# Local attention: V evicted on VectorE, q's norm as the exponential's per-row scale, the input split on POOL

## What is computed

```python
def _layer(x, wqkv, qs, ksc, wo, lg, lb, w1, b1, w2, b2):
    h = shift_token(x)
    q, k, v = jnp.split(h @ wqkv, 3, axis=-1)       # 8 heads of 64
    q = l2norm(q) * qs
    k = l2norm(k) * ksc
    q, k = rotary_xpos(q, k)
    o = local_attention(q, k, v)                    # windows of 64, each with the one before it
    x = x + o @ wo
    h = layernorm(shift_token(x)) * lg + lb
    h = h @ w1 + b1
    a, g = jnp.split(h, 2, axis=-1)
    return x + (a * gelu(g)) @ w2 + b2
```

## Time and profile before

| | |
|---|---|
| median of 3 runs | 910.92 us (910.48 to 911.56) |
| the profiled execution's own time | 909.12 us |
| its span on the core | 907.3 us |
| mean granted TensorE clock | 0.98 of full speed |
| busy: TensorE, VectorE, ScalarE, POOL | 89%, 75%, 71%, 59% |
| local loop, 27 passes of layer 1 | 208.58 to 430.86 us |
| local loop, 27 passes of layer 2 | 567.89 to 790.16 us |

### The profile page before, as it was taken

The page is one execution under the profiler, slowest core; times in us unless marked ns, Lnnn a source line. Parts: engine busy times, 40 slices in busy tenths (PEclk is TensorE's granted clock), DMA queues, the critical chain, the costliest instruction groups (busy, mean ns, idle before and its releaser), DMA issues.

```text
span 907.3 us, 26209 instructions
## 1 busy us (share of the span) xinstructions
PE 803.8 (89%) x9912; PEld 616.1 (68%) x9912; DVE 677.0 (75%) x1389; ACT 645.5 (71%) x2037; POOL 531.6 (59%) x529
## 2 busy tenths in 40 slices
PE   4979999779999999999889887999999999988985
PEld 3558777557777777778766555777877777775652
DVE  4788898777887887787466767778787788746765
ACT  1217677579989899889743237988988998964463
POOL 1494233178888888888610008888888888951100
PEclk9999999989999999999999999999999999999998
DMA  7220001012222222222201122222222222222001
GB/s 272 73 52 4 3 4 41 3 48 54 51 64 57 60 51 63 53 63 54 60 19 24 23 52 54 63 55 57 58 61 56 62 51 61 57 51 100 0 35 58
DMA packets 64704, 48.24 MB, mean 53 GB/s; under 512 B 40410, under 2 KB 50948, under 8 KB 64068
## 3 DMA queue, kind: packets, MB, share of 16 engines
q1 hardware_dynamic: 64580, 46.57, 19.9%
HBM read 10.63 MB, written 2.10 MB: 14 GB/s over the span
## 4 chain that ended last, share of the span: by engine, by line
PE 55%; DVE 17%; ACT 17%; issue 7%; POOL 2%; DMA 1%; SPq 0%; DVEq 0%; POOLq 0%; ACTq 0%
PE ps L404 46%; PE ps L414 9%; ACT prob L862 6%; DVE nmax L1124 3%; ACT sq L804 3%; DVE nt L1152 2%; ACT V L831 2%; ACT oT L813 2%; DVE split L952 2%; ACT kT L838 1%; ACT pT L808 1%; DVE prob L1211 1%; DVE split L950 1%; ACT qT L823 1%; DVE vexp L1043 1%
## 5 line engine op out<-in xcount | busy, mean ns | idle before, releaser
L862 ACT ACTIVATE prob<-ps,nmax 128x128 f32<-128x128 f32 x512 | 181.8, 375 | 35.6 <-DVE nmax L1124 35.5
L404 PE MATMUL ps<-wqkv,split 128*128 128x512 f32 x576 | 186.8, 435 | 13.4 <-DVE split L952 9.9
L1349 POOL TENSOR_TENSOR prob<-prob,rinv 128x512 f32<-128x512 f32 x128 | 133.7, 1045 | 87.2 <-DVE rinv L1110 45.8
L404 PEld LDWEIGHTS ps<-wqkv,split 128*128 128x128 f32 x576 | 96.9, 194 | 32.5 <-DVE split L952 10.0
L1124 DVE TENSOR_REDUCE nmax<-ps 128x4 f32<-128x512 f32 x128 | 83.6, 686 | 47.0 <-PE ps L404 47.0
L414 PE MATMUL ps<-ident,prob 128*128 128x128 f32 x640 | 97.8, 276 | 14.1 <-POOL prob L1349 13.2
L862 ACT ACTIVATION_READ_ACCUMULATOR prob<-ps,nmax 128x1 f32 x512 | 109.2, 213 | 0.0
L1360 POOL TENSOR_TENSOR qr<-qr,ss 128x512 f32<-128x512 f32 x64 | 66.9, 1045 | 52.1 <-DVE qr L1136 52.1
L414 PEld LDWEIGHTS ps<-ident,prob 128*128 128x128 f32 x640 | 75.6, 141 | 28.3 <-POOL prob L1349 17.5
L404 PE MATMUL ps<-oT,wo 128*128 128x128 f32 x512 | 73.9, 287 | 22.2 <-ACT oT L813 22.2
L404 PEld LDWEIGHTS ps<-oT,wo 128*128 128x128 f32 x512 | 62.1, 191 | 37.5 <-ACT oT L813 36.5
(11 more groups left out here) (134 smaller groups left out, 1886.3 us busy)
## 6 DMA issues: line engine op xcount, KB each, us to landing
VB<-V SPq DMA_DIRECT2D x129, 128.0 KB, 2.4
kT<-kT SPq DMA_DIRECT2D x65, 128.0 KB, 2.4
XS<-X SPq DMA_DIRECT2D x32, 128.0 KB, 2.3
XS<-X SPq DMA_DIRECT2D x128, 32.0 KB, 1.9
D<-in_xT SPq DMA_DIRECT2D x8, 256.0 KB, 4.9
XS<-in_xT SPq DMA_DIRECT2D x2, 1024.0 KB, 6.3
out_T<-XS SPq DMA_DIRECT2D x8, 256.0 KB, 2.0
raw<-in_wqkv SPq DMA_DIRECT2D x2, 768.0 KB, 3.9
```

Of the source, the lines that this page charges most:

```text
L404: return nc.tensor.matmul(o, l, r, start=start, stop=stop, skip_group_check=True)
L862: nc.scalar.activation(prob[:, par, grp, s * P:(s + 1) * P], ps[:, 4 + grp, s * P:(s + 1) * P], ACT.Exp, bias=nmax[:, par, grp * 4 + s:grp ...
L1349: g.tensor_tensor(p4, p4, rinv[:, slot, 4 * grp:4 * grp + 4].unsqueeze(2).broadcast_to([P, 4, P]), ALU.mult).then_inc(l_prob, 1)
```

## The change

Three things are done together.

1. V's eviction from PSUM bank 2 goes from ScalarE to VectorE. On VectorE it stands behind the sums of squares and ahead of the maxima.
2. The rotated q is no longer multiplied by its inverse norm on POOL. The scores are then those of the unscaled q. The inverse norm, one number a row and head, is given to each exponential as a per-row scale; the negated maximum has to be scaled as well, which is a new VectorE product of 128x4 (`scaled_maxima`) behind each maximum. `ss` gets a third slot, and TensorE's turn of q waits for VectorE's q directly.
3. The input is split per tile of 128 tokens on POOL, at the end of each pass, and no more per chunk of 512 on VectorE every fourth pass.

```diff
 (TensorE)
-                        pe.wait_ge(l_split, L * CHUNKS + (n + 2) // TPC + 1)
+                        pe.wait_ge(l_split, base + n + 3)
...
-                        transposed(n, par, qr, l_qn)
+                        transposed(n, par, qr, l_qr)
 (ScalarE)
-                    if live(n, 0, TILES):
-
-                        act.wait_ge(l_v, base + n + 1)
-                        wait(act, l_o, base + n - 1)
-                        if live(n, -1, TILES):
-                            act.wait_ge(v_prev[nxt], 32 * ((base + n - 1) // 2 + 1))
-                        nc.scalar.activation(V[:, par, :], ps[:, 2, :], ACT.Copy).then_inc(l_ve, 1)
...
-                            wait(act, l_qn, base + n + 1)
-                            wait(act, l_kn, base + n + 1)
-                            nc.scalar.activation(ss[:, par, :], lognt[:, 1, :], ACT.Exp, scale=-0.5).then_inc(l_rnorm, 1)
+                            wait(act, l_kn, base + n)
+                            wait(act, l_max, 2 * (base + n))
+                            nc.scalar.activation(ss[:, (n + 2) % 3, :], lognt[:, 1, :], ACT.Exp, scale=-0.5).then_inc(l_rnorm, 1)
...
                                                      bias=nmax[:, par, grp * 4 + s:grp * 4 + s + 1],
+                                                     scale=ss[:, n % 3, 2 * s + grp:2 * s + grp + 1],
 (VectorE)
-                            v.tensor_reduce(nmax[:, par, 4 * grp:4 * grp + 4],
+                            v.tensor_reduce(rawmax[:, par, 4 * grp:4 * grp + 4],
                                             ps[:, 4 + grp, :].rearrange("p (s k) -> p s k", s=4),
-                                            AX_X, ALU.max, negate=True).then_inc(l_max, 1)
+                                            AX_X, ALU.max, negate=True).then_inc(l_rawmax, 1)
+
+                    def scaled_maxima(grp):
+                        if live(n, 0, TILES):
+                            dve.wait_ge(l_rawmax, 2 * (base + n) + grp + 1)
+                            v.tensor_tensor(nmax[:, par, 4 * grp:4 * grp + 4], rawmax[:, par, 4 * grp:4 * grp + 4],
+                                            ss[:, n % 3, grp:HEADS:2], ALU.mult).then_inc(l_max, 1)
...
+                    if live(n, 0, TILES):
+                        dve.wait_ge(l_v, base + n + 1)
+                        wait(dve, l_o, base + n - 1)
+                        if live(n, -1, TILES):
+                            dve.wait_ge(v_prev[nxt], 32 * ((base + n - 1) // 2 + 1))
+                        v.tensor_copy(V[:, par, :], ps[:, 2, :]).then_inc(l_ve, 1)
                     maxima(0)
-                    if live(n, 3, TILES) and (n + 3) % TPC == 0:
-                        j = (n + 3) // TPC
-                        if j > 1:
-                            dve.wait_ge(l_v, base + n + 3 - TPC)
-                        split_into(j % 2, shifted(XS[0], j, CHUNK), CHUNK, l_split, L * CHUNKS + j)
+                    scaled_maxima(0)
                     maxima(1)
+                    scaled_maxima(1)
 (POOL)
-                        pool.wait_ge(l_qr, base + n + 2)
-                        pool.wait_ge(l_rnorm, base + n + 2)
-                        g.tensor_tensor(hd(qr[:, nxt, :]), hd(qr[:, nxt, :]),
-                                        ss[:, nxt, 0:8].unsqueeze(2).broadcast_to([P, HEADS, HD]),
-                                        ALU.mult).then_inc(l_qn, 1)
...
+                    if live(n, 3, TILES):
+                        m = n + 3
+                        wait(pool, l_v, base + m - 2 * TPC + 1)
...
+                        x_m, slot, cols = shifted(XS[0], m, P), (m // TPC) % 2, bass.ds((m % TPC) * P, P)
+                        g.tensor_copy(split[:, slot, 0, cols], x_m).then_inc(split_hi, 1)
+                        pool.wait_ge(split_hi, base + m + 1)
+                        g.tensor_tensor(split[:, slot, 1, cols], x_m, split[:, slot, 0, cols].bitcast(F32),
+                                        ALU.subtract).then_inc(l_split, 1)
```

More of the change, by code:

```diff
@@ L134, in build @@
         VB = sb("VB", [P, 2, INNER])
-        ss = sb("ss", [P, 2, 2 * HEADS])
+        ss = sb("ss", [P, 3, 2 * HEADS])
+        rawmax = sb("rawmax", [P, 2, HEADS])
         nt = sb("nt", [P, 2 * HEADS])
@@ L235, in build @@
         l_qr = sem("l_qr")
-        l_qn = sem("l_qn")
+        l_rawmax = sem("l_rawmax")
         l_kr = sem("l_kr")
@@ L945, in rstd_links @@
                     ins.then_inc(ln_rstd, 1)
[L947 to L952, removed]
             def centre(base, j, src, bank):
@@ L1131, in local @@
                         v.tensor_tensor(hd(kn[:]), hd(ps[:, 1, :]),
-                                        ss[:, nxt, 8:16].unsqueeze(2).broadcast_to([P, HEADS, HD]),
+                                        ss[:, (n + 1) % 3, 8:16].unsqueeze(2).broadcast_to([P, HEADS, HD]),
                                         ALU.mult).then_inc(l_kn, 1)
@@ L1371, in local @@
                         g.tensor_tensor(kr[:, nxt, :], kA[:], kB[:], ALU.add).then_inc(l_kr, 1)
+                    if live(n, 3, TILES):
+                        m = n + 3
+                        wait(pool, l_v, base + m - 2 * TPC + 1)
+                        if m == 0:
+                            pool.wait_ge(xs_dma, xs_before_local(0) if L == 0 else xs_before_ffn(L - 1) + 32)
+                            wait(pool, ffn_a, NPART * (L * CHUNKS - 1))
+                        elif m == TPC:
+                            pool.wait_ge(xs_dma, xs_before_local(L))
+                            wait(pool, ffn_a, NPART * L * CHUNKS)
+                        x_m, slot, cols = shifted(XS[0], m, P), (m // TPC) % 2, bass.ds((m % TPC) * P, P)
[3 more added lines that the diff above has]
+                                        ALU.subtract).then_inc(l_split, 1)
                     if live(n, 0, TILES):
                         normalise(n, par, 0)
-                steps(-1, TILES - 2, local)
+                steps(-3, TILES - 2, local)
                 local(TILES - 1, 1)
```

## The result

The changed kernel takes 1185.95 us in the median (1180.02 to 1191.21, four runs) against 910.7 us; the ratio is 1.302, with a 95% interval of 1.294 to 1.311. The profiled execution took 1180.02 us, its span is 1178.2 us and its mean granted TensorE clock 0.90.

A forecast was written before the change was run, and what follows sets the result against it. The local-attention loop was taken as bound by TensorE's work and ScalarE's list in turn, 8.23 us a pass; the new one-pass loop sums to 11.47. 909.1 + 194 + 4 + 36 = 1143, 1145 at the median; range 1065 to 1195.

The forecast's parts named there:

- rival (c): In the local-attention loop the TensorE clock falls in nearly every pass: 1180 to 1265 us; chance 0.15.
- maxima to exponentials: Loop step from the maxima's start to the first exponential, with the new product by q's norm: 0.90 us a pass.
- exponentials: Loop step on ScalarE: eight exponentials with an added per-row scale, and the small one: 3.58 us for 2.86.
- first square to second square, over q's eviction and the turn of k: Loop step through ScalarE's squares and evictions and TensorE's turn of k: 2.30 us a pass.
- second square to third product: Loop step over VectorE's norm reduction and V's eviction, up to TensorE's projection of V: 2.01 us a pass.
- third product to VectorE: Loop step on TensorE: projection of V, second turn of the probabilities, scores reaching VectorE: 2.68 us a pass.
- rival (a): The one-pass loop as forecast, but the TensorE clock never falls: 1109 us; chance 0.2.
- The clock: Idle piece before the third product sometimes lowers TensorE's clock: 0.6 us a pass, +36 us, bounds 0 and 156.
- Rival (b): The exponential's second per-row operand is fetched for nothing: 1066 us without, 1102 with the clock's share; chance 0.12.
- Rival (d): V is evicted early enough that bank 2 is free in time: 906 us, 884 with the scale for nothing; chance 0.02.
- the old two-tile loop would stay: With bank 2 free in time, TensorE's work and ScalarE's list still alternate over two tiles: 16.27 us, 8.14 a tile.
- Nothing else reaches this loop: In the local-attention loop, VectorE's other work and oT's eviction have room to spare and add no time.

The follow-up runs named there:

- e3: Changed kernel with eight more, unneeded TensorE products a pass between the turn of k and the third product: 1109.11 us, ratio 1.219.
- e4: Kernel before with only V's eviction moved to VectorE behind the reductions: 1132.20 us, ratio 1.243.
- e1: Changed kernel with VectorE's eviction of V moved ahead of the rotation products: 964.75 us, ratio 1.060.
- e6: Kernel before with only q's norm as the exponential's per-row scale and the products of the maxima: 966.71 us, ratio 1.062.
- e5: Changed kernel with q's scale back on POOL, without the exponential's per-row scale and the maxima's product: 1132.35 us, ratio 1.245.
- e7: Kernel before with only the split per tile on POOL, q's scale staying on POOL: 926.44 us, ratio 1.018.
- e9: Kernel before with the split per tile on VectorE, behind the addition to X: 915.96 us, ratio 1.0066.
- e11: Kernel before with V evicted early on VectorE, oT's eviction before second turned probabilities, per-tile split: copy on ScalarE, subtraction on VectorE; 899.01 us, 0.9894.
- e2: Changed kernel with V's eviction back on ScalarE where it was: 971.69 us, ratio 1.067.

## Why the prediction was right, and where it was off

The direction, the place and the mechanism were right, and the time lies in the range (1065 to 1195), but outside the forecast's own range (1120 to 1170). The forecast was 1145; 1186 lies in the range of rival (c), the clock falling in nearly every pass, though it fell in only 41 of 57.

*The loop.* The terms, predicted and measured at full clock: maxima to exponentials 0.90 and 0.93; exponentials 3.58 and 3.60; first square to second square, over q's eviction and the turn of k, 2.30 and 2.35; second square to third product 2.01 and 1.96; third product to VectorE 2.68 and 2.67 (426.93 to 429.60). The sum was 11.47 and is 11.51, which is also what every pass of e3 takes. V's eviction took 682 ns, as the row from PSUM had it. e3 confirms the total too: with the clock kept up 1109 us, the 1109 of rival (a).

*The count.* The wait occurs 60 times, as predicted.

*The clock is the term that was mis-sized.* I put 0.6 us a pass and 36 us, by taking one of two idle pieces to be followed by a low clock and half of the 2.6 us of work behind it to be covered, 1.3 us. Measured: 12.76 us a pass in layer 1 and 12.50 in layer 2, less 11.51, so 1.1 us a pass and 67 us in the profiled execution, which is 66 us longer than that of e3; between the medians it is 77. Both factors were low. The clock fell in 41 of 57 passes, 0.72 and not 0.5, and a pass in which it fell lost 1.6 us on average. The two stretches of the old trace were weak ground for either factor. They are single, they contradict each other, and neither holds a piece of 2.5 us, though the prediction calls both "such a piece". TensorE's timeline of the kernel before has the two:

```profile
194.15 0.66 PE L414 MATMUL ps<-ident,prob 128*128 128x128 f32 x4 [2.36 <-POOL prob L1349]
201.47 0.96 PE L404 MATMUL ps<-wqkv,split 128*128 128x512 f32 x3 [1.98 <-DVE split L952]
```

The clock stayed up after the longer piece and fell after the shorter one, so the length of one piece does not tell whether it falls. Why it fell in 41 passes of the changed kernel and not in 16 with the same idle piece, and in nearly every pass of e4, stays open. Rival (c) had the right size, 70 to 156 us, with a chance of only 0.15. The upper bound of the range, 1195, is worked out from no term; that 1186 came in 9 us under it is partly luck.

*Rival (b)* is out by the 460 ns. *Rival (d)*, bank 2 free in time, was priced wrongly: it gave 906 us, and e1, which is that kernel, took 965. The step at fault is "the old two-tile loop would stay". The scale lengthens the way from the maxima to q's eviction until the turn of k waits for it, and this closes a loop of one pass, in which a microsecond on ScalarE costs a whole one and not half. The same error priced the scale at half (e6).

*Nothing else reaches this loop* holds for the changed kernel. The split and POOL, costed at nothing, cost nothing there (e4 against e5), but only because the wait covers them: without it POOL's split costs 17 us (e7). The three parts alone cost 222, 57 and 17 us, together 297, against 275 for the whole: the split's 17 are hidden in the long pass, and the scale costs 54 there and not 57.

## What to carry to other kernels

An eviction frees a PSUM bank for the next product. In the evicting engine's queue it should stand ahead of operations that wait for TensorE's work of the same pass just before that product; behind them, TensorE stands still for the whole length of that chain. A wait that is charged with no idle time may be met with only 0.05 us in hand. An idle piece that recurs in each pass should be priced with the low clock in most passes, and the range should reach up to all of them. A saving is "worth half" only as long as no shorter loop has closed. Moving work to another engine pays when the new place is free at that time, which the timelines of both engines show and the busy shares do not.

## What the runs showed of the hardware

- Idle pieces of 2.5 us, one in each pass, let TensorE's clock fall to 1.2 GHz in 41 of 57 passes: in layer 1 the loop had 0.86 in the mean over passes of 12.76 us; with 1.7 us of the piece filled (e3) it was at 0.99.
- Small VectorE operations on SBUF took longer beside POOL's rotation of k: 0.49 us for 0.16 (a product of 128x4, e1), 0.82 us (a copy of 128x128, e9) and 1.21 us for 0.29 (a subtraction of 128x128, e11). They end 0.02, 0.07 and 0.16 us behind POOL's operation. In e2, where POOL's ends at 336.72, the product of 128x4 starts at 336.35, takes 0.39 us and ends at 336.74. The addition to X, which has one operand in PSUM, took its usual 0.28 us beside the same operation of POOL (e11, 306.48). That the ports are the cause rests on these ends and was not tested by itself.
- A second per-row operand of an exponential costs 85 ns (375 to 460 ns). The eight in a row with the small one took 3.60 us for 2.86, and all of that was on the path.
